# First attention layer: the sums over the keys as two rounded passes, both halves in the second step of the next batch

## The chip, the cores and the metric

The kernel runs on one core of one Trainium2 chip. TensorE (PE in the profile) multiplies matrices, VectorE (DVE), ScalarE (ACT) and GpSimd (POOL) do the elementwise work, and SyncE (SP) starts the transfers. Each engine takes its instructions in the order in which they are written, and engines wait for each other through semaphores. The metric is the device time of one execution in microseconds. Time before: 2079.07 us, the median of 3 runs (2076.28 to 2079.29).

## What is computed

The reference is a block of two layers on x of shape (16, 56, 256) with a context of shape (16, 1500, 128). Only the first cross attention matters here. For each of 16 batches, with 16 heads of 56 queries and 1500 keys:

```python
q = (layernorm(x) @ Wq).reshape(B, T_text, 16, 128)
k, v = context @ Wk, context @ Wv
attn = softmax(where(mask, q @ k.T / sqrt(128), -inf))   # over the 1500 keys
x = x + (attn @ v) @ Wo
```

The softmax divides by the sum of the exponentials over the keys. That sum is what the change is about. After this attention come a small mixing layer, a second cross attention and a mixture of experts.

## The kernel before

The loop over the batches `b` (16) has 12 steps `t` each. A step handles a tile of 125 keys against 896 query columns (16 heads of 56), in two halves of 448 columns. PSUM has three score banks in rotation (`slots`), three banks for side work (`side`) and two for the values (`psO`).

In step `t` of batch `b`:

- TensorE makes the scores of the next tile, `t + 1` (`scores_half`, L792 to L795): per half four matmuls of rounded operands (type F32R). Score operands are split in a high part (rounded, `chi`, `qhi`) and a low part (`clo`, `qlo`), and a fourth matmul adds the shift (`ones_r` by `shift`), which takes the largest score off. Then it multiplies the exponentials `P` of tile `t` by the context (`values_half`, L804, plain F32).
- Between these stand side jobs, in a fixed order: M (L826, scores of the batch after, for its maximum), T (transposes of it), N and A (L842 and L843, products from which the norms of the keys for the second layer are made). A side job may start only when the job three before it has been taken out of its bank by VectorE.
- ScalarE turns each half of the scores into exponentials (`exp`, L570), squares up the A jobs (`add_up`, L552, four pairs of instructions a job), rounds the operands of the batch after (`query_high`, `context_high`), and copies out the values of a batch at its end (`values_out`, L577).
- GpSimd adds the exponentials of the tiles up in `acc` (`add`, L641 for the first pair and L644), makes low parts (`context_low`, `query_low`), halves the N jobs (`halve`, L650), makes the shift of the batch after in step 10 (`make_shift`), and normalises (`normalise`, L657).
- VectorE takes M, T, N and A out of their banks (L711, L714, L738), adds up N (L747) and inverts the sums in steps 3 to 10 (`invert`, L753).

`acc` holds 125 partial sums for each query column. Over the 125 partitions TensorE adds them with a matmul by ones (`sums`, L812), plain F32, one for each half, and ScalarE copies the result to `den` (`sums_out`, L583). For batch `b - 1` this is done in batch `b`: the first half in step 0 behind the scores, the second at the head of step 1. On ScalarE the first copy stands in step 0 behind the exponentials, and the second behind the first A job of step 0. GpSimd's first `add` of batch `b` waits until both have been made, since it writes `acc` anew.

`ORDER` is the rotation of the three score banks, written out by hand: "S" stands for the scores of a step and half, "D" for the sums of the batch before, and "-" for a place left free. A bank is taken again three places later, and `wait_bank` makes TensorE wait for the reader of the place before: an exponential or a copy of a sum. The dispatch of ScalarE in a batch begins:

```python
for tile in tile_ahead(1, b, t):
    exp(*tile)
if t == 0 and b > 0:
    sums_out(b - 1, 0)
    norms_out(b - 1)
```

and goes on, through the conversions of the batch after where a step has them, to that step's A jobs.

Of the kernel before, what the change touches and what calls it, by code (L numbers as in the profile page):

```python
# [88 lines left out]
ORDER = [("S", 0, 0), ("S", 0, 1), ("S", 1, 0), ("S", 1, 1), ("D", 0, 0), ("D", 0, 1), ("-", 0, 0)]  # L89
ORDER += [("S", t, half) for t in range(2, NT) for half in range(2)]  # L90
# [66 lines left out]
def before_attention(nc, m, a, tag, sem):  # L157

    s = semaphores(sem, tag, LN_SEMAPHORES + ["ld_x", "ld_mask", "ld_const", "ld_ident", "ld_w0", "ld_w0_rest", "ld_wq0", "ld_wq1", "ld_wq2", "ld_wq3", "ld_w1", "ld_land", "ld_nat", "const", "ready",
                 "on_act", "on_dve", "f_hi", "g_hi", "x_hi", "mcount", "ctx_hi", "q_hi", "ctx_lo", "kept",  # L160
                 "side_pe", "side_dve"])
    with ExitStack() as ctx:
# [88 lines left out]
        def _(pool):  # L251
# [5 lines left out]
            pool.tensor_tensor(m.qlo0[:, :], q_first, m.qhi0[:, :].bitcast(F32), ALU.subtract).then_inc(s.kept, 1)  # L257
# [9 lines left out]
        def _(dve):  # L267
# [40 lines left out]
            def make_shift():  # L308

                dve.wait_ge(s.side_dve, len(PRE_SIDE))  # L310
                dve.wait_ge(s.ld_ident, 16)
                dve.tensor_tensor(m.shift0[:, :].rearrange("p (j c) -> p j c", c=TT),
                                  m.negmax[:, :].unsqueeze(2).to_broadcast([TT, QBLK, TT]),
                                  m.ident[0:TT, 0:TT].unsqueeze(1).to_broadcast([TT, QBLK, TT]),
                                  ALU.mult).then_inc(s.kept, 1)
# [125 lines left out]
def first_attention(nc, m, a, tag, sem):  # L441
# [3 lines left out]
        "scores", "probs", "pv", "acc", "den", "den_out", "inv", "o_raw", "o_done",  # L445
        "ld_wv", "ld_wo", "side_pe", "side_dve", "side_act", "half_sum", "sum_dve", "sum_act", "rk_pre"])
    NP = 3
    with ExitStack() as ctx:
# [12 lines left out]
        shift = [m.shift0, sb("shift1", [TT, QW], F32R)]  # L461
# [60 lines left out]
        def _(act):  # L522
# [55 lines left out]

            def sums_out(b, half):

                act.wait_ge(s.den, 2 * b + half + 1)
                need(act, s.o_done, 2 * b - 1 + half)
                act.activation(den[:, half, :], bank_of("D", 0, half)[:, 0:HALF], ACT.Copy).then_inc(s.den_out, 1)  # L583
# [5 lines left out]
            for b in range(B):  # L589
                for t in range(NT):  # L590
                    for tile in tile_ahead(1, b, t):
                        exp(*tile)
                    if t == 0 and b > 0:
                        sums_out(b - 1, 0)
                        norms_out(b - 1)
# [6 lines left out]
                    for n in STEP_JOBS[b, t]:  # L602
                        if JOBS[n].kind == "A":
                            add_up(n)
                        if n == first_of(b, "A") and b > 0:
                            sums_out(b - 1, 1)
# [14 lines left out]
        def _(pool):  # L621
# [7 lines left out]
            def query_low(b):  # L629
                pool.wait_ge(s.q_hi, b)  # L630
                if b >= 2:
                    pool.wait_ge(s.scores, 2 * NT * (b - 1))
                pool.tensor_tensor(qlo[b % 2][:, :], m.qs[:, b, :, :].rearrange("p h q -> p (h q)"),
                                   qhi[b % 2][:, :].bitcast(F32), ALU.subtract).then_inc(s.q_lo, 1)

            def add(b, t):
                pool.wait_ge(s.probs, 2 * (NT * b + t + 1))
                if t == 1:

                    need(pool, s.den, 2 * b)  # L640
                    pool.tensor_tensor(acc[:, :], P[0][:, :], P[1][:, :], ALU.add).then_inc(s.acc, 1)  # L641
                else:
                    pool.wait_ge(s.acc, (NT - 1) * b + t - 1)
                    pool.tensor_tensor(acc[:, :], acc[:, :], P[t % NP][:, :], ALU.add).then_inc(s.acc, 1)  # L644

# [22 lines left out]
            def make_shift(b):  # L668
# [3 lines left out]
                pool.tensor_tensor(shift[b % 2][:, :].rearrange("p (j c) -> p j c", c=TT),  # L672
# [4 lines left out]
            for b in range(B):  # L677
                for t in range(NT):
# [15 lines left out]
                    for n in STEP_JOBS[b, t]:  # L694
                        if JOBS[n].kind == "N":
                            halve(n)
            normalise(B - 2, 1)
# [4 lines left out]
        def _(dve):  # L702
# [13 lines left out]
            def turn_max(n):  # L716
# [3 lines left out]
                need(dve, s.shift, b - 1)  # L720
# [61 lines left out]
        def _(pe):  # L782
            def scores_half(b, t, half):
                if half == 0 and t == 0:
                    need(pe, s.ctx_lo, NLOW * b)
                    need(pe, s.q_lo, b)
                    need(pe, s.shift, b)
# [7 lines left out]
                pe.matmul(out, m.ones_r[:, :], shift[b % 2][:, cols], start=False, stop=True).then_inc(s.scores, 1)  # L795
# [12 lines left out]
            def sums(b, half):  # L808

                pe.wait_ge(s.acc, (NT - 1) * (b + 1))  # L810
                wait_bank(pe, b + 1, "D", 0, half)
                pe.matmul(bank_of("D", 0, half)[:, 0:HALF], m.ones[0:KT, :], acc[:, HALF * half:HALF * half + HALF],  # L812
                          start=True, stop=True).then_inc(s.den, 1)
# [34 lines left out]
            for b in range(B):  # L848
                for t in range(NT):
# [1120 lines left out]
def build(nc, a, out):  # L1970
    with ExitStack() as ctx:
# [26 lines left out]
        with ExitStack() as only:  # L1998
            for_first = lambda n, sh, dt: only.enter_context(nc.sbuf_tensor(n, sh, dt))
            m.ones_r = for_first("ones_r", [TT, KT], F32R)  # L2000
# [7 lines left out]
            m.shift0 = for_first("shift0", [TT, QW], F32R)  # L2008
# [54 lines left out]
```

## Time and profile before

| what | value |
|---|---|
| median of 3 runs | 2079.07 us |
| profiled execution, its own time | 2075.8 us |
| its span, first to last instruction | 2074.0 us |
| TensorE busy | 2044.6 us (99%) |
| VectorE, ScalarE, GpSimd busy | 1567.0, 1209.1, 1452.1 us |
| granted TensorE clock, mean | 0.999 |
| batches of the first attention | from 73 to about 1159 us |

In rows with times, the first number is the start from the beginning of the span and the second the duration, both in us; a bracket at the end gives the idle time of the engine before the row and what ended it. Matmuls overlap, so what one costs the stream is the time from its start to the start of the next, not its duration. A plain F32 matmul is recorded as two; the first of its records starts when it starts, and the instruction behind it appears early, so its cost is read over the following two starts.

### The profile page before, as it was taken

The page shows a single profiled execution, that of the slowest core. Times are in us where ns is not written, and L with a number is a line of the kernel's source. Part 1 is how long each engine was busy: PE and PEld are TensorE (multiplying, and loading weights), DVE is VectorE, ACT ScalarE, POOL GpSimd, SP SyncE. Part 2 cuts the span into 40 slices and gives each one's busy share as a digit, 9 for nine tenths or more (in the row PEclk, how much of TensorE's full clock was granted, in tenths as well). Part 3 has the DMA queues.
Part 4 walks back from the last instruction along what each step waited for, and adds up shares of the span by engine and source line. Part 5 has one row for each costly group of instructions (what it writes and reads, how often), then busy time and mean ns, then how long its engine had stood idle before and what let it go on. Part 6 is the DMA issues. An engine that isn't in the chain of part 4 may idle for free. (4 is left out here: it accounts for less than half of the span.)

```text
span 2074.0 us, 28056 instructions
## 1 busy us (share of the span) xinstructions
PE 2044.6 (99%) x8414; PEld 1511.9 (73%) x8414; DVE 1567.0 (76%) x2466; ACT 1209.1 (58%) x4202; POOL 1452.1 (70%) x1092
## 2 busy tenths in 40 slices
PE   8999999999999999999999999999999999999999
PEld 7777777777777777777777577666666666665898
DVE  4788988998889888988886677576766676752576
ACT  3676777777776777677767347544444444432443
POOL 1588888888888888888896255578787878761221
PEclk9999999999999999999999999999999999999999
DMA  4000000000000000000000320221212121101110
GB/s 138 31 16 16 31 30 16 26 21 31 29 18 16 31 30 16 16 31 30 16 16 36 121 74 1 63 60 31 60 30 60 30 60 30 45 1 54 39 54 26
DMA packets 16472, 76.59 MB, mean 37 GB/s; under 512 B 1986, under 2 KB 3506, under 8 KB 15314
## 3 DMA queue, kind: packets, MB, share of 16 engines
q1 hardware_dynamic: 16322, 74.81, 11.1%
q8 instruction: 67, 1.10, 0.2%
q14 instruction: 83, 0.68, 0.1%
HBM read 72.97 MB, written 0.92 MB: 36 GB/s over the span
## 5 line engine op out<-in xcount | busy, mean ns | idle before, releaser
L552 ACT ACTIVATE l_prod_act<-l_prod_act 125x128 f32<-125x128 f32 x1536 | 456.3, 299 | 298.3 <-DVE l_prod_act L738 293.3
L650 POOL TENSOR_TENSOR l_prod<-l_prod 125x256 f32<-125x256 f32 x384 | 280.8, 740 | 162.9 <-DVE l_prod L738 161.7
L1014 POOL TENSOR_TENSOR l_acc<-l_acc,l_probs 125x896 f32<-125x896 f32 x160 | 346.7, 2167 | 67.8 <-ACT l_probs L951 49.4
L951 ACT ACTIVATE l_probs<-l_scaled 125x896 f32<-125x896 f32 x192 | 182.8, 952 | 302.6 <-DVE l_scaled L1036 160.5
L1036 DVE TENSOR_TENSOR l_scaled<-l_slots,rk 125x896 f32<-125x896 f32 x192 | 206.9, 1084 | 180.8 <-PE l_slots L1112 180.7
L644 POOL TENSOR_TENSOR l_acc<-l_acc,l_probs 125x896 f32<-125x896 f32 x160 | 340.1, 2126 | 0.0
L552 ACT ACTIVATION_READ_ACCUMULATOR l_prod_act<-l_prod_act 125x1 f32 x1536 | 288.0, 187 | 0.0
L714 DVE SCALAR_TENSOR_TENSOR top<-l_side,mask_bias,top 125x448 f32<-125x448 f32 x330 | 217.6, 659 | 25.7 <-PE l_side L826 17.3
L570 ACT ACTIVATE l_probs<-l_slots,mask_bias 125x448 f32<-125x448 f32 x384 | 219.8, 618 | 1.2
L1110 PE MATMUL l_slots<-l_qhi,l_clo 128*125 128x448 f32 x384 | 203.0, 529 | 0.5
L842 PE MATMUL l_side<-norm_lo,l_chi 128*125 128x512 f32 x384 | 185.1, 482 | 0.1
L842 PE MATMUL l_side<-norm_lo,chi 128*125 128x512 f32 x384 | 180.9, 471 | 0.0
L804 PE MATMUL l_psO<-l_probs,spare 125*128 125x448 f32 x384 | 176.0, 539 | 0.0
L804 PE MATMUL l_psO<-l_probs,l_nat 125*128 125x448 f32 x384 | 175.9, 539 | 0.0
L738 DVE TENSOR_TENSOR l_prod<-l_side,xq 125x512 f32<-125x512 f32 x192 | 132.0, 687 | 50.6 <-PE l_side L843 48.9
L738 DVE TENSOR_TENSOR l_prod<-l_side,spare 125x512 f32<-125x512 f32 x192 | 132.0, 687 | 39.7 <-PE l_side L843 37.1
L1128 PE MATMUL l_psO<-l_probs,nat 125*128 125x448 f32 x384 | 160.5, 539 | 0.6 <-ACT qs L963 0.3
L1128 PE MATMUL l_psO<-l_probs,l_nat 125*128 125x448 f32 x384 | 160.3, 540 | 0.4
L747 DVE TENSOR_REDUCE l_msq<-l_prod 125x4 f32<-125x256 f32 x384 | 154.5, 409 | 0.0
L843 PE MATMUL l_side<-norm_hi,chi 128*125 128x512 f32 x384 | 151.4, 394 | 0.0
L843 PE MATMUL l_side<-norm_hi,l_chi 128*125 128x512 f32 x384 | 151.3, 394 | 0.0
L1111 PE MATMUL l_slots<-l_qlo,l_chi 128*125 128x448 f32 x384 | 140.5, 366 | 0.0
(278 smaller groups left out, 4926.0 us busy)
## 6 DMA issues: line engine op xcount, KB each, us to landing
land<-in_ctxT SPq DMA_DIRECT2D x32, 750.0 KB, 4.2
l_nat<-in_ctxN SPq DMA_DIRECT2D x16, 750.0 KB
post_we<-in_experts SPq DMA_DIRECT2D x20, 384.0 KB, 3.0
spare<-in_ctxN SPq DMA_DIRECT2D x8, 750.0 KB
nat<-in_ctxN SPq DMA_DIRECT2D x8, 750.0 KB
spare<-in_wo SPq DMA_DIRECT2D x2, 2048.0 KB, 7.3
spare<-in_wqT SPq DMA_DIRECT2D x4, 512.0 KB, 8.4
mid_fac<-in_factors SPq DMA_DIRECT2D x1, 2048.0 KB, 7.5
```

The costliest lines, as they stand in the source:

```text
L552: last = act.activation(whole, whole, ACT.Copy, accum_out=msq[:, t, 4 * g + c:4 * g + c + 1])
L570: act.activation(P[t % NP][:, HALF * i:HALF * i + HALF], bank_of("S", t, i)[0:KT, 0:HALF], ACT.Exp, bias=m.mask_bias[:, b, t:t + 1]).then_ ...
L644: pool.tensor_tensor(acc[:, :], acc[:, :], P[t % NP][:, :], ALU.add).then_inc(s.acc, 1)
L650: pool.tensor_tensor(buf[:, :, 0:C // 2], buf[:, :, 0:C // 2], buf[:, :, C // 2:C], ALU.add).then_inc(s.half_sum, 1)
L714: dve.scalar_tensor_tensor(top[:, cols], bank, bias, top[:, cols], ALU.add, ALU.max).then_inc(s.side_dve, 1)
L738: dve.tensor_tensor(to[:, :, :], bank, xt.unsqueeze(1).to_broadcast([KT, 4, C]), ALU.mult).then_inc(s.side_dve, 1)
L804: last = pe.matmul(psO[:, half, 0:HALF], nat[b % 2][:, t, :], P[t % NP][:, cols], start=t == 0, stop=t == NT - 1)
L842: pe.matmul(bank[0:KT, :], chi[b % 2][:, keys], m.norm_lo[:, cols], start=True, stop=False)
L843: last = pe.matmul(bank[0:KT, :], chi[b % 2][:, keys], m.norm_hi[:, cols], start=False, stop=True)
L1014: pool.tensor_tensor(acc[:, :], acc[:, :], P[t % NP][:, :], ALU.add).then_inc(s.acc, 1)
L1036: dve.tensor_tensor(scaled[t % 2][:, :].rearrange("p (a h q) -> p a h q", a=2, q=QS), src, rk.to_broadcast([KT, 2, H // 2, QS]), ALU.mult) ...
L1128: last = pe.matmul(psO[:, half, 0:HALF], nat[par][:, t, :], P[t % NP][:, cols], start=t == 0, stop=t == NT - 1)
```

## The change

The sums are made from rounded operands in two passes. ScalarE rounds `acc` to a high part (`sum_high`) into the buffer `qlo` of the batch just done; GpSimd takes the difference (`sum_low`) into that batch's `shift` buffer, which grows from 112 to 125 rows. TensorE adds ones by low and ones by high, in type F32R. Both halves are made one behind the other in step 1 behind the scores of tile 2, and ScalarE copies both out behind the exponentials of tile 2. `ORDER` has the two sums behind the scores of step 2. The last batch's sums stay as they were.

```diff
-ORDER = [("S", 0, 0), ("S", 0, 1), ("S", 1, 0), ("S", 1, 1), ("D", 0, 0), ("D", 0, 1), ("-", 0, 0)]
-ORDER += [("S", t, half) for t in range(2, NT) for half in range(2)]
+ORDER = [("S", t, half) for t in range(3) for half in range(2)] + [("D", 0, 0), ("D", 0, 1), ("-", 0, 0)]
+ORDER += [("S", t, half) for t in range(3, NT) for half in range(2)]
...
-        shift = [m.shift0, sb("shift1", [TT, QW], F32R)]
+        shift = [m.shift0, sb("shift1", [KT, QW], F32R)]
...
+            def sum_high(b):
+
+                act.wait_ge(s.acc, (NT - 1) * (b + 1))
+                act.wait_ge(s.scores, 2 * NT * (b + 1))
+                act.activation(qlo[b % 2][0:KT, :], acc[:, :], ACT.Copy).then_inc(s.sum_hi, 1)
...
                     for tile in tile_ahead(1, b, t):
                         exp(*tile)
+                    if t == 1 and b > 0:
+                        for half in range(2):
+                            sums_out(b - 1, half)
                     if t == 0 and b > 0:
-                        sums_out(b - 1, 0)
+                        sum_high(b - 1)
                         norms_out(b - 1)
...
                         if JOBS[n].kind == "A":
                             add_up(n)
-                        if n == first_of(b, "A") and b > 0:
-                            sums_out(b - 1, 1)
...
                 if b >= 2:
                     pool.wait_ge(s.scores, 2 * NT * (b - 1))
+                    pool.wait_ge(s.den, 2 * (b - 1))
...
                 if t == 1:
-
-                    need(pool, s.den, 2 * b)
+                    need(pool, s.shift, 2 * b)
                     pool.tensor_tensor(acc[:, :], P[0][:, :], P[1][:, :], ALU.add).then_inc(s.acc, 1)
...
+            def sum_low(b):
+
+                pool.wait_ge(s.sum_hi, b + 1)
+                pool.tensor_tensor(shift[b % 2][:, :], acc[:, :], qlo[b % 2][0:KT, :].bitcast(F32), ALU.subtract).then_inc(s.shift, 1)
...
                 need(pool, s.scores, 2 * NT * (b - 1))
-                pool.tensor_tensor(shift[b % 2][:, :].rearrange("p (j c) -> p j c", c=TT),
+                need(pool, s.den, 2 * (b - 1))
+                pool.tensor_tensor(shift[b % 2][0:TT, :].rearrange("p (j c) -> p j c", c=TT),
...
                     for n in STEP_JOBS[b, t]:
                         if JOBS[n].kind == "N":
                             halve(n)
+                    if t == 0 and b > 0:
+                        sum_low(b - 1)
...
-                need(dve, s.shift, b - 1)
+                need(dve, s.shift, 2 * b - 3)
...
-                    need(pe, s.shift, b)
+                    need(pe, s.shift, 2 * b - 1)
...
-                pe.matmul(out, m.ones_r[:, :], shift[b % 2][:, cols], start=False, stop=True).then_inc(s.scores, 1)
+                pe.matmul(out, m.ones_r[0:TT, 0:KT], shift[b % 2][0:TT, cols], start=False, stop=True).then_inc(s.scores, 1)
...
-                pe.wait_ge(s.acc, (NT - 1) * (b + 1))
+                cols, out = slice(HALF * half, HALF * half + HALF), bank_of("D", 0, half)[:, 0:HALF]
                 wait_bank(pe, b + 1, "D", 0, half)
-                pe.matmul(bank_of("D", 0, half)[:, 0:HALF], m.ones[0:KT, :], acc[:, HALF * half:HALF * half + HALF],
-                          start=True, stop=True).then_inc(s.den, 1)
+                if b == B - 1:
+                    pe.wait_ge(s.acc, (NT - 1) * B)
+                    pe.matmul(out, m.ones[0:KT, :], acc[:, cols], start=True, stop=True).then_inc(s.den, 1)
+                    return
+                pe.wait_ge(s.shift, 2 * b + 2)
+                pe.matmul(out, m.ones_r[0:KT, :], shift[b % 2][:, cols], start=True, stop=False)
+                pe.matmul(out, m.ones_r[0:KT, :], qlo[b % 2][0:KT, cols], start=False, stop=True).then_inc(s.den, 1)
...
-                    if t == 1 and b > 0:
-                        sums(b - 1, 1)
                     for half in range(2):
                         for tile in tile_ahead(1, b, t):
                             scores_half(*tile, half)
-                        if half == 1 and t == 0 and b > 0:
+                        if half == 1 and t == 1 and b > 0:
                             sums(b - 1, 0)
+                            sums(b - 1, 1)
                         side_jobs(len(jobs) // (4 - half))
```

`ones_r` grows to 128 by 128, and `shift0` to 125 rows (of which the maker of the first shift writes 112); a semaphore that nothing waited for (`kept`) goes.

## Rows read from the trace of the kernel before

**Rows 1.** Busy time by stretch, batches of the first attention; (x) counts instructions

```profile
73.00:1159.00 1086.00, 1085.84 (x4422) 814.03 (x4421) 942.51 (x1665) 781.19 (x3587) 904.52 (x800) 1.00 0.07 24
```

**Rows 2.** Timeline of TensorE, end of batch 1 and steps 0 and 1 of batch 2

```profile
208.31 0.37 PE L792 MATMUL l_slots<-qhi,clo 128*125 128x448 f32 x1
...
209.13 0.92 PE L812 MATMUL l_slots<-l_acc,ones 125*128 125x448 f32 x2
209.54 0.71 PE L826 MATMUL l_side<-l_qhi,l_chi 128*125 128x448 f32 x1
210.09 0.40 PE L842 MATMUL l_side<-norm_lo,chi 128*125 128x512 f32 x1
...
210.55 0.92 PE L804 MATMUL l_psO<-l_probs,spare 125*128 125x448 f32 x2
...
213.40 0.92 PE L812 MATMUL l_slots<-l_acc,ones 125*128 125x448 f32 x2
...
216.48 0.37 PE L826 MATMUL l_side<-l_qhi,l_chi 128*125 128x448 f32 x1
```

**Rows 3.** Timeline of ScalarE over the same stretch, from its last wait on

```profile
207.80 0.31 ACT L552 ACTIVATE l_prod_act<-l_prod_act 125x128 f32<-125x128 f32 x1 [0.25 <-DVE l_prod_act L738]
...
208.99 0.99 ACT L577 ACTIVATE qs<-l_psO,valid 128x896 f32<-128x896 f32 x1
...
211.95 0.53 ACT L583 ACTIVATE l_den<-l_slots 128x448 f32<-128x448 f32 x1
212.38 0.36 ACT L559 ACTIVATE rk<-l_msq 125x192 f32<-125x192 f32 x1
212.83 0.31 ACT L552 ACTIVATE l_prod_act<-l_prod_act 125x128 f32<-125x128 f32 x1
...
214.35 0.55 ACT L583 ACTIVATE l_den<-l_slots 128x448 f32<-128x448 f32 x1 [0.24 <-PE l_slots L812]
214.79 0.30 ACT L552 ACTIVATE l_prod_act<-l_prod_act 125x128 f32<-125x128 f32 x1
...
215.96 1.36 ACT L570 ACTIVATE l_probs<-l_slots,mask_bias 125x448 f32<-125x448 f32 x2
```

**Rows 4.** Timeline of ScalarE: a rounding copy of 896 columns and the next start

```profile
205.04 0.94 ACT L526 ACTIVATE l_qhi<-qs 128x896 fp32r<-128x896 f32 x1
205.88 0.51 ACT L535 ACTIVATE l_chi<-land 128x375 fp32r<-128x375 f32 x1
```

**Rows 5.** Groups by line and shape, ScalarE, batches of the first attention

```profile
L570 ACT ACTIVATE l_probs<-l_slots,mask_bias 125x448 f32<-125x448 f32 x384 | 219.8, 618 | 1.2
```

**Rows 6.** Timeline of all engines at the head of batch 0: a wait of TensorE

```profile
74.05 1.17 ACT L570 ACTIVATE l_probs<-l_slots,mask_bias 125x448 f32<-125x448 f32 x2
...
74.74 0.18 PEld L792 LDWEIGHTS l_slots<-qhi,clo 128*125 128x125 f32 x1 [0.41 <-ACT l_probs L570]
74.74 0.47 PE L792 MATMUL l_slots<-qhi,clo 128*125 128x448 f32 x1
...
75.04 0.36 PE L793 MATMUL l_slots<-qlo,chi 128*125 128x448 f32 x1
```

**Rows 7.** Timeline of VectorE and GpSimd over the same steps, in order of time

```profile
210.29 0.68 DVE L711 TENSOR_SCALAR top<-l_side,mask_bias 125x448 f32<-125x448 f32 x1 [0.35 <-PE l_side L826]
...
212.31 0.68 DVE L738 TENSOR_TENSOR l_prod<-l_side,spare 125x512 f32<-125x512 f32 x1
...
213.07 0.73 POOL L650 TENSOR_TENSOR l_prod<-l_prod 125x256 f32<-125x256 f32 x1 [2.31 <-DVE l_prod L738]
...
214.46 2.12 POOL L641 TENSOR_TENSOR l_acc<-l_probs 125x896 f32<-125x896 f32 x1 [0.66 <-PE l_slots L812]
...
219.69 0.73 POOL L650 TENSOR_TENSOR l_prod<-l_prod 125x256 f32<-125x256 f32 x1 [1.46 <-DVE l_prod L738]
```

**Rows 8.** Timeline of TensorE, ScalarE and GpSimd, steps 0 and 1 of batch 15

```profile
1089.22 0.99 PE L804 MATMUL l_psO<-l_probs,l_nat 125*128 125x448 f32 x2
...
1090.01 0.54 ACT L583 ACTIVATE l_den<-l_slots 128x448 f32<-128x448 f32 x1
...
1091.55 0.73 POOL L650 TENSOR_TENSOR l_prod<-l_prod 125x256 f32<-125x256 f32 x1 [2.29 <-DVE l_prod L738]
...
1094.58 0.40 PE L842 MATMUL l_side<-norm_lo,l_chi 128*125 128x512 f32 x1
```

More of the change, by code:

```diff
@@ L159, in before_attention @@
     s = semaphores(sem, tag, LN_SEMAPHORES + ["ld_x", "ld_mask", "ld_const", "ld_ident", "ld_w0", "ld_w0_rest", "ld_wq0", "ld_wq1", "ld_wq2", "ld_wq3", "ld_w1", "ld_land", "ld_nat", "const", "ready",
-                 "on_act", "on_dve", "f_hi", "g_hi", "x_hi", "mcount", "ctx_hi", "q_hi", "ctx_lo", "kept",
+                 "on_act", "on_dve", "f_hi", "g_hi", "x_hi", "mcount", "ctx_hi", "q_hi", "ctx_lo",
                  "side_pe", "side_dve"])
@@ L256, in _ @@
             pool.wait_ge(s.q_hi, 1)
-            pool.tensor_tensor(m.qlo0[:, :], q_first, m.qhi0[:, :].bitcast(F32), ALU.subtract).then_inc(s.kept, 1)
+            pool.tensor_tensor(m.qlo0[:, :], q_first, m.qhi0[:, :].bitcast(F32), ALU.subtract)
             pool.wait_ge(s.q_hi, 2)
@@ L311, in make_shift @@
                 dve.wait_ge(s.ld_ident, 16)
-                dve.tensor_tensor(m.shift0[:, :].rearrange("p (j c) -> p j c", c=TT),
+                dve.tensor_tensor(m.shift0[0:TT, :].rearrange("p (j c) -> p j c", c=TT),
                                   m.negmax[:, :].unsqueeze(2).to_broadcast([TT, QBLK, TT]),
                                   m.ident[0:TT, 0:TT].unsqueeze(1).to_broadcast([TT, QBLK, TT]),
-                                  ALU.mult).then_inc(s.kept, 1)
+                                  ALU.mult)
             dve.memset(m.ones[:, :], 1.0).then_inc(s.const, 1)
@@ L444, in first_attention @@
         "ld_land", "ld_nat0", "ld_nat1", "ctx_hi", "ctx_lo", "q_hi", "q_lo", "nat_hi", "xq", "shift",
-        "scores", "probs", "pv", "acc", "den", "den_out", "inv", "o_raw", "o_done",
+        "scores", "probs", "pv", "acc", "sum_hi", "den", "den_out", "inv", "o_raw", "o_done",
         "ld_wv", "ld_wo", "side_pe", "side_dve", "side_act", "half_sum", "sum_dve", "sum_act", "rk_pre"])
@@ L1999, in build @@
             for_first = lambda n, sh, dt: only.enter_context(nc.sbuf_tensor(n, sh, dt))
-            m.ones_r = for_first("ones_r", [TT, KT], F32R)
+            m.ones_r = for_first("ones_r", [C, C], F32R)
             m.mask_bias = for_first("mask_bias", [KT, B, NT], F32)
@@ L2007, in build @@
             m.top, m.negmax = for_first("top", [KT, QW], F32), for_first("negmax", [TT, QBLK], F32)
-            m.shift0 = for_first("shift0", [TT, QW], F32R)
+            m.shift0 = for_first("shift0", [KT, QW], F32R)
             m.xq = for_first("xq", [KT, NT, C], F32)
```

## The prediction

> **What bounds the kernel now.** I read the busy times by stretch first. Over the first attention's batches TensorE is busy 1085.84 of 1086.00 us at full clock, the other engines far less [rows 1]. So what is taken off TensorE's stream is gained, and whatever makes it wait is lost, as long as it stays the bound. The stream's costs come from starts. Four F32R matmuls of 448 columns take from 208.31 to 209.13, 0.205 us each. The plain F32 sum with one such matmul behind it takes from 209.13 to 210.09, so a sum costs 0.96 - 0.205 = 0.755 us [rows 2]. It is made 32 times, and 30 of them change.
>
> Then I read ScalarE's timeline at a batch's head, since the new order hangs on it. ScalarE last waits, 0.25 us for an A job, before the `add_up` at 207.80. That job comes from TensorE, so ScalarE's place is tied to TensorE's there. From there to 214.11 ScalarE goes without a pause: `values_out` and the conversions of the batch after have put it behind [rows 3]. Slack that its share of busy time suggests is absent at this one place. The heads of batches 1 to 14 run to the same pattern; batch 15 is calmer, as nothing is converted ahead.
>
> **The change, part by part.** I follow batch 2's head on the clock of before; TensorE has finished step 1's second score half at 216.48, both old sums included [rows 2]. That is the point to compare.
>
> *TensorE's work.* Two F32 sums (1.51 us) go. Four F32R matmuls (0.82 us) come. The gain in work is 0.69 us a head, 10.4 us over 15 heads.
>
> *Order on TensorE.* Without the old sums it would be at that point at 216.48 - 1.51 = 214.97. It would reach the values of tile 0 at 210.55 - 0.755 = 209.80. They need `values_out`, which ends at 208.99 + 0.99 = 209.98 [rows 2, 3]. What a wait costs is shown once: ScalarE's first exponential ends at 74.05 + 0.62 = 74.67, TensorE's matmul behind it starts at 74.74, and the next not after 0.205 but after 0.30 us [rows 5, 6]. So 0.07 us from end to start and 0.10 us of weight load laid bare. The values start effectively at 209.98 + 0.17 = 210.15, 0.35 us late, and the sums' place is reached at 215.32. The Trainium skill, page "TensorE: Matmul & The Clock Gate", section on the array's architecture, says that TensorE's queue pulls weight loads ahead of matmuls in flight. If it did so past a wait, the 0.10 us would vanish; the row at 74.74 shows load and matmul starting together, so the sum keeps it. By that rule the sum would end some 1.5 us lower.
>
> *The first half's wait: the low part.* `sum_high` starts on ScalarE where the first copy stood, 211.95. Its like, `query_high`, takes 0.94 us and lets the next start after 0.84 [rows 4]. It ends at 212.89. GpSimd comes to `sum_low` behind the second `halve` of step 0, at 213.07 before, released by VectorE's product at 212.31 [rows 7]. TensorE is 0.40 us early there, but VectorE has only 0.35 us of waiting to give back in that step [rows 7], so the halving moves to about 212.7 and ends the engine's turn at 213.4. `sum_low` is a GpSimd operation on 125x896 like `add`, 2.12 us [rows 7]: done at 215.5. TensorE makes the first half from 215.6 to 216.1 (0.30 + 0.205).
>
> *The second half's wait: its bank.* By the new `ORDER` the second sum goes into the bank of the scores of tile 2, first half, and `wait_bank` holds it until that exponential is out. On ScalarE that exponential stands behind both A jobs of step 0. Before, it started at 215.96. In between go the first copy (212.38 - 211.95 = 0.43 us) and the second with its wait (214.79 - 214.00 = 0.79; at 212.83 + 1.17 = 214.00 the first `add_up` would let the next start), together 1.22 us; `sum_high` brings 0.84 [rows 3, 4]. The 1.17 us of one `add_up` is 215.96 - 214.79. So it starts at 215.96 - 0.38 = 215.58 and its first half ends at 215.58 + 0.62 = 216.20 [rows 3, 5]. TensorE resumes at 216.27, with 0.30 + 0.205 us for the pair: 216.78. Against 216.48 the head is 0.30 us longer than before. TensorE has lost 0.35 us, then about 0.3 for the low part and about 0.3 for the bank and bare loads, more than the 0.69 gained.
>
> Behind the waiting matmul stand all side jobs and the values of step 1, so VectorE and the A jobs of ScalarE wait too. It can't be made up, because TensorE never idles later.
>
> *What is free.* GpSimd gets 2.12 us a head and loses a wait of 0.66; its first `add` ends near 217.5 instead of 216.6, and the 1.46 us of waiting before 219.69 takes that up [rows 7]. The first exponential that needs this `add` is that of tile 3, a whole step on. Were the cover gone, step 2's halvings would slip by about 1 us, and VectorE uses them three N jobs later. The two copies on ScalarE end near 217.5 (216.20 + 0.52 for the second exponential, then twice 0.43), and step 1's first A job comes behind a pair of score matmuls, an M job and its own product only after that. The bank of the first sum is asked for again by the scores of tile 3, in the next step. The new waits on `den` and `shift` in `query_low`, `make_shift` and `turn_max` look back most of a batch. The larger buffers and memsets cost nothing inside the loop. No transfer is added, and no load waits on anything that moves here.
>
> *Batch 15.* Before, TensorE's values wait for `values_out` already (0.99 where 0.92 is usual), so taking the first sum away there gives nothing; the point to compare is 1094.58 [rows 8]. GpSimd's halving at 1091.55 stays, `sum_low` runs from 1092.28 to 1094.40, the first half to 1094.97. ScalarE: 1090.01 + 0.84 + 0.45 + 1.17 = 1092.47, the second `add_up` 1.17 more, with 0.24 us for a wait of the kind in [rows 3]: 1093.88, so the exponential ends at 1094.5, in time. The second half ends at 1094.97 + 0.41 = 1095.38. That is 0.8 us longer.
>
> *Sum.* 14 x 0.30 + 0.8 = 5.0 us. On the profiled execution: span 2074.0 to 2079.0, its own time 2075.8 to 2080.8, 1.8 us above the span as before. The median of before lies 3.3 us above that execution; I add the 5.0 to the median: 2084.1 us, up 0.24%.
>
> **Bounds.** ScalarE's wake-up of TensorE costs from nothing to 0.17 plus the longest exposure that rows allow, a whole weight load of 0.18 in place of 0.10 [rows 6]: -0.17 to +0.08 a head, which gives 14 x 0.13 + 0.6 = 2.4 at the low end and 14 x 0.38 + 0.9 = 6.2 at the high end. The mean is near the shown case, which I take. `sum_low` has no row of its own; the nearest are `add` at 2.12 and the halving at 0.73. With 0.3 us more it would put the first half's end at 216.4, and the pair would end at about 216.8 all the same. With 1 us more the head grows by 0.5, another 7 us over the heads.
>
> **The rivals.**
>
> *The bank is free in time* (0.10). If the exponential of tile 2 did not hold the second sum, only the low part would: the pair ends at 216.1 + 0.205 = 216.3, 0.18 us before 216.48. 14 x -0.18 + 0.8 = -1.7: 2077.4 us, not slower. It decides from an exponential that ends before about 215.9, 0.3 us earlier than I have it. For it speaks only that the two copies leave ScalarE's step 0. Against it: both `add_up` still stand ahead, and no wait but 0.24 us was left on ScalarE there [rows 3].
>
> *The work saved is the time saved* (0.08). TensorE waits for nothing: -10.4 us, 2068.7. It needs the low part 0.6 us and the exponential 1.2 us earlier. For it: 99% of TensorE busy. Against: every row of the sum above.
>
> *The low part comes late* (0.08). `sum_low` beside VectorE's reads takes longer, or ScalarE's `sum_high` does and pushes the exponential: each 0.2 us beyond the margin is 0.2 a head, 15 x 0.2 = 3.0 us, so 2084.1 + 3.0 = 2087.1 us. For it: both are new in a stretch where ScalarE has no slack. Against: the same forms keep their durations elsewhere, 0.94 and 2.12 us.
>
> *TensorE's weight loads run ahead past the wait* (0.12). The head is 0.20 us longer, batch 15 0.7: 3.5 us, 2082.6, under the bound below. [...]
>
> **How the numbers follow.** The forecast has 0.62. A measurement of this kernel tells apart about 0.2%, 4.2 us. The forecast's own range, 2.4 to 6.2 us with the scatter of the runs (3 us between them) on top, lies about two thirds above 4.2. Slower by more than 0.2%: 0.62 x 0.70 + 0.08 + 0.12 x 0.3 = 0.55. Faster by more than 0.2%: the second rival, and a fifth of the first, 0.10. The rest, 0.35, is within 0.2%. The range 2077 to 2088 reaches to the first rival and to the late low part, and leaves out the second.
>
> **What would show it.** In the changed profile: F32R matmuls of the sums in pairs of 0.205 us; a wait of TensorE before the values of tile 0 on ScalarE's `values_out`, one before the first sum on GpSimd's low part, and one before the second sum on the exponential of tile 2, all told about 1.0 us a head where there was none. From one batch's head to the next it takes 0.3 us longer. TensorE busy falls by about 10 us while the span grows. GpSimd's wait for the sums is gone. If there is no wait on the exponential, the first rival holds. It would be wrong at large if ScalarE's work at the head ran otherwise than in these rows, or if the later end of step 1 were made up by something that waited for VectorE until now.

## The result and the profile after

The changed kernel takes 2081.36 us (median of 20 runs, 2079.53 to 2086.95) where the kernel before takes 2078.99 (20 runs). The ratio of the two is 1.0022, with a 95% interval of 1.0016 to 1.0028: slower by 4.6 us of 2079, and forecast were 5.0. The two medians themselves lie only 2.4 us apart, and the forecast median was 2084.1. The times go with the mean granted clock of the execution: of the changed kernel's 20, the four at 1.000 take 2079.5 to 2080.4 us and the three at 0.996 take 2084.8 to 2087.0; the kernel before, timed again beside e1 below, has five at 1.000 from 2073.6 to 2074.9, so at equal clock about 5.6 us lie between. The profiled execution has a span of 2080.9 us against 2074.0, 6.9 us more; that difference holds 1.7 us that are not the change's, see below.

The timeline of the changed kernel at the head of batch 2, the place of [rows 2], [rows 3] and [rows 7] (sum lines: L583 is now the rounding copy, L656 the low part, L832 and L833 the two passes, L846 the M job, L862 the first product of an N or A job, L819 the values, L726 VectorE taking an M job out of its bank):

```profile
208.31 0.30 ACT L552 ACTIVATE l_prod_act<-l_prod_act 125x128 f32<-125x128 f32 x1
...
209.83 0.31 ACT L552 ACTIVATE l_prod_act<-l_prod_act 125x128 f32<-125x128 f32 x1 [0.25 <-DVE l_prod_act L753]
...
211.02 0.99 ACT L577 ACTIVATE qs<-l_psO,valid 128x896 f32<-128x896 f32 x1
...
211.42 0.18 PEld L862 LDWEIGHTS l_side<-norm_lo,chi 128*125 128x125 f32 x1 [0.28 <-DVE top L726]
...
212.15 0.99 PE L819 MATMUL l_psO<-l_probs,spare 125*128 125x448 f32 x2
...
213.97 0.95 ACT L583 ACTIVATE l_qlo<-l_acc 125x896 fp32r<-125x896 f32 x1
...
215.44 2.13 POOL L656 TENSOR_TENSOR l_shift<-l_acc,l_qlo 125x896 fp32r<-125x896 f32 x1
...
217.18 0.36 PE L810 MATMUL l_slots<-shift,ones_r 112*125 112x448 f32 x1
...
217.63 1.13 ACT L570 ACTIVATE l_probs<-l_slots,mask_bias 125x448 f32<-125x448 f32 x2
...
217.72 2.12 POOL L648 TENSOR_TENSOR l_acc<-l_probs 125x896 f32<-125x896 f32 x1
217.72 0.44 PE L832 MATMUL l_slots<-l_shift,ones_r 125*128 125x448 f32 x1 [0.18 <-POOL l_shift L656]
...
218.00 0.36 PE L833 MATMUL l_slots<-l_qlo,ones_r 125*128 125x448 f32 x1
218.29 0.19 PEld L832 LDWEIGHTS l_slots<-l_shift,ones_r 125*128 125x128 f32 x1 [0.30 <-ACT l_probs L570]
218.29 0.47 PE L832 MATMUL l_slots<-l_shift,ones_r 125*128 125x448 f32 x1
218.40 0.19 PEld L833 LDWEIGHTS l_slots<-l_qlo,ones_r 125*128 125x128 f32 x1
218.60 0.37 PE L833 MATMUL l_slots<-l_qlo,ones_r 125*128 125x448 f32 x1
...
218.80 0.37 PE L846 MATMUL l_side<-l_qhi,l_chi 128*125 128x448 f32 x1
```

To lay this beside the rows of before, take the point to which ScalarE is tied, its last wait for an A job: 209.83 here, 207.80 there [rows 3]. Everything here is 2.03 us later for reasons that lie before this head. Taken off:

| step of the prediction | forecast | measured less 2.03 |
|---|---|---|
| values of tile 0 start, behind `values_out` | 210.05, and 0.10 for the bare load | 210.12 in the record |
| rounding copy on ScalarE | 211.95 | 211.94 |
| low part on GpSimd, start and time | 213.4, 2.12 | 213.41, 2.13 |
| the sums' place reached on TensorE | 215.32 | 215.36 (217.18 + 0.205) |
| first sum on TensorE | 215.6 | 215.69 |
| exponential of tile 2 on ScalarE | 215.58 | 215.60 |
| second sum on TensorE | 216.27 | 216.26 |
| the stream goes on | 216.78 | 216.77 |

Before, it went on at 216.48 [rows 2]. A head is 0.29 us longer although TensorE has 0.69 us less to do.

The waits of the changed kernel, over the first attention's batches; columns are the total, the number of times and the longest. They hold all three waits of the prediction, 14 or 15 times each, and one more, for VectorE (L726):

```profile
PEld l_slots L832 <- issue: 8.3, 15, 0.9
PEld l_psO L819 <- issue: 6.7, 15, 1.0
...
PEld l_slots L832 <- ACT l_probs L570: 4.2, 14, 0.3
PEld l_side L862 <- DVE top L726: 4.0, 14, 0.3
...
PE l_slots L832 <- POOL shift L656: 1.3, 7, 0.2
PE l_slots L832 <- POOL l_shift L656: 1.2, 7, 0.2
```

A lesson in reading stands here. TensorE's wait before the first sum is put down mostly to "issue", and its matmul row to only 0.18 us, because the matmuls before it are recorded as overlapping. The honest measure is again from start to start: the last score matmul starts at 217.18 and would let the next start at 217.39; it starts at 217.72.

**Where the 6.9 us of the span lie.** GpSimd's `make_shift` runs once a batch, late in it. These are its first and last in one buffer, of the kernel before and of the changed one (first and last start at the end):

```profile
L672 POOL TENSOR_TENSOR l_shift<-negmax,ident x8: 1682/1685/1685, 130.5 to 1077.2; 112x896 fp32r<-112x896 f32 x8
```

```profile
L685 POOL TENSOR_TENSOR l_shift<-negmax,ident x8: 1679/1680/1686, 132.2 to 1083.2; 112x896 fp32r<-112x896 f32 x8
```

Between them lie the heads of batches 1 to 14: 951.0 us for 946.7, so 4.3 us or 0.31 a head. At 132.2 the changed kernel is already 1.7 us late, before it has made a single sum. That is TensorE's clock in the preparation, and it is a property of the execution. Of the 1.7 us, 1.6 lie in one run of 24 products, recorded as 2.94 us before and 4.57 after. Its rows, before and after:

```profile
21.38 2.94 PE L406 MATMUL pre_bk<-pre_wkT 128*128 128x128 f32 x24 [0.94 <-DVE pre_fold_lo L348]
```

```profile
21.49 4.57 PE L406 MATMUL pre_bk<-pre_wkT 128*128 128x128 f32 x24 [0.94 <-DVE pre_fold_lo L348]
```

Busy times of the same stretch, before and after (the number behind POOL's count is the granted clock):

```profile
18.00:24.30 6.30, 4.09 (x34) 3.89 (x34) 6.20 (x21) 3.73 (x8) 0.00 (x0) 1.00 0.55 198
```

```profile
18.00:24.30 6.30, 3.96 (x22) 3.77 (x23) 6.19 (x20) 3.13 (x7) 0.00 (x0) 0.79 0.53 202
```

A mean of 0.79 says that for part of the stretch the lower of the two clock levels, 1.2 GHz, was granted (from 22 to 24 us the mean is 0.50): 22 matmuls for 34. From 18 to 22 us TensorE had been busy 1.67 us in this execution and 1.79 us in that of before, whose clock stayed. Other executions below start the attention's first matmul at 71.2 to 72.9 us, whatever the kernel; e4's starts it at 72.59 with a clock of 1.00 in this stretch, so a late start is not the clock each time. So I compare profiles by the stretch of the attention alone, from its first score matmul to the first of its closing matmuls. Before and after:

```profile
71.41 0.44 PE L792 MATMUL l_slots<-qhi,clo 128*125 128x448 f32 x1 [1.10 <-PEq L162]
```

```profile
L875 PE MATMUL l_side<-qs,spare x32: 537/539/542, 1154.7 to 1166.3; 128*128 128x448 f32 x32
```

```profile
73.11 0.44 PE L807 MATMUL l_slots<-qhi,clo 128*125 128x448 f32 x1 [1.09 <-PEq L162]
```

```profile
L894 PE MATMUL l_side<-qs,spare x32: 538/539/542, 1161.6 to 1173.2; 128*128 128x448 f32 x32
```

1083.3 us before, 1088.5 after: 5.2 us longer, 5.0 were forecast. Of these 4.3 are the fourteen heads, and 0.9 is left for batch 15, where 0.8 was forecast. The rows there, changed kernel:

```profile
1095.26 0.99 PE L819 MATMUL l_psO<-l_probs,l_nat 125*128 125x448 f32 x2 [0.60 <-ACT qs L577]
...
1098.28 2.14 POOL L656 TENSOR_TENSOR shift<-l_acc,qlo 125x896 fp32r<-125x896 f32 x1
...
1101.46 0.40 PE L862 MATMUL l_side<-norm_lo,l_chi 128*125 128x512 f32 x1
```

The values start 6.04 us behind those of before (1089.22), and the job behind the sums 6.88 us (1094.58) [rows 8]: 0.84 us longer, nearly all of it the wait for the low part, which is done at 1098.28 + 2.14 = 1100.42.

### The profile page after: what moved, and what is told of

It is laid out like the page before. It is cut to its first block and busy times, and to the rows that moved or that the text cites. A ratio compares the mean times of both kernels' runs of the same rounds, so it can differ in the third digit from the quotient of the medians.

```text
span 2080.9 us, 28101 instructions
## 1 busy us (share of the span) xinstructions
PE 2048.9 (98%) x8414; PEld 1510.9 (73%) x8414; DVE 1565.1 (75%) x2466; ACT 1218.1 (59%) x4217; POOL 1482.5 (71%) x1107
## 5 line engine op out<-in xcount | busy, mean ns | idle before, releaser
L862 PE MATMUL l_side<-norm_lo,l_chi 128*125 128x512 f32 x384 | 185.7, 483 | 0.1
L862 PE MATMUL l_side<-norm_lo,chi 128*125 128x512 f32 x384 | 181.5, 473 | 0.0
L819 PE MATMUL l_psO<-l_probs,l_nat 125*128 125x448 f32 x384 | 176.5, 540 | 0.6 <-ACT qs L577 0.6
L819 PE MATMUL l_psO<-l_probs,spare 125*128 125x448 f32 x384 | 176.5, 541 | 0.0
L753 DVE TENSOR_TENSOR l_prod<-l_side,xq 125x512 f32<-125x512 f32 x192 | 131.8, 687 | 50.7 <-PE l_side L863 49.0
L753 DVE TENSOR_TENSOR l_prod<-l_side,spare 125x512 f32<-125x512 f32 x192 | 131.8, 686 | 39.8 <-PE l_side L863 37.2
```

The lines of the kernel that those rows point to most:

```text
L753: dve.tensor_tensor(to[:, :, :], bank, xt.unsqueeze(1).to_broadcast([KT, 4, C]), ALU.mult).then_inc(s.side_dve, 1)
L819: last = pe.matmul(psO[:, half, 0:HALF], nat[b % 2][:, t, :], P[t % NP][:, cols], start=t == 0, stop=t == NT - 1)
L862: pe.matmul(bank[0:KT, :], chi[b % 2][:, keys], m.norm_lo[:, cols], start=True, stop=False)
```

## The experiments

Nine more kernels ran, one of them twice (e10 is e3 again), each timed over five rounds. Ratios are to the kernel before; the stretch is taken from each kernel's profile in the way just shown. Where a mean change per head is given, it comes from the starts of `make_shift`, again as above, over the fourteen heads.

| kernel | ratio, 95% interval | stretch, us | against before |
|---|---|---|---|
| before | 1 | 1154.7 - 71.41 = 1083.3 | |
| changed | 1.0022, 1.0016 to 1.0028 | 1161.6 - 73.11 = 1088.5 | +5.2 |
| e1, both sums later | 0.9972, 0.9963 to 0.9981 | 1152.0 - 72.67 = 1079.3 | -4.0 |
| e2, second sum later | 1.0011, 1.0002 to 1.0019 | 1157.2 - 71.37 = 1085.8 | +2.5 |
| e4, the place alone | 1.0021, 1.0012 to 1.0029 | 1161.9 - 72.59 = 1089.3 | +6.0 |
| e5, `values_out` ahead | 0.9989, 0.9981 to 0.9998 | 1155.3 - 72.90 = 1082.4 | -0.9 |
| e3, both edits | 0.9951, 0.9938 to 0.9963 | 1146.4 - 71.18 = 1075.2 | -8.1 |
| e6, kernel before, `values_out` ahead | 0.9997, 0.9988 to 1.0006 | 1154.7 - 71.41 = 1083.3 | 0.0 |
| e7, more on ScalarE | 1.0087, 1.0074 to 1.0099 | 1172.4 - 71.57 = 1100.8 | +17.5 |
| e8, more on ScalarE with both edits | 0.9967, 0.9955 to 0.9979 | 1146.5 - 71.17 = 1075.3 | -8.0 |
| e9, maxima first | 0.9968, 0.9956 to 0.9980 | 1148.6 - 71.55 = 1077.1 | -6.2 |
| e10, both edits again | 0.9952, 0.9939 to 0.9965 | 1146.6 - 71.41 = 1075.2 | -8.1 |

### e1: both sums later

```diff
                         if half == 1 and t == 1 and b > 0:
-                            sums(b - 1, 0)
-                            sums(b - 1, 1)
                         side_jobs(len(jobs) // (4 - half))
                     values_half(b, t, 0)
+                    if t == 1 and b > 0:
+                        sums(b - 1, 0)
+                        sums(b - 1, 1)
```

(The emptied `if` goes too.)

> The changed kernel with both sums moved on TensorE behind the first half of the values of step 1, some 1.4 us later; ScalarE and GpSimd as in the change. Theory A (TensorE's waits at the head eat the gain: 0.35 us on values_out, about 0.3 on the low part, about 0.3 on the bank held by the exponential of tile 2): the last two waits are gone, the first stays. 0.69 gained less 0.35 lost is 0.34 us a head over 14 heads, batch 15 level: about -4.7 us against the kernel before, ratio 0.9977, and 9.6 us under the changed kernel. Rival B (the added work itself costs: the rounding copy on ScalarE and the difference on GpSimd hold up side jobs): the move changes nothing, ratio near 1.002. Rival C (copies of the sums on ScalarE come later and push its add_up): slower than the changed kernel.

0.9972 and 4.0 us less in the stretch. The waits for the low part and for the bank are what cost; the passes themselves, ScalarE's rounding copy and GpSimd's difference are all still there, and the kernel is faster than before. Rival B falls. Rival C too: ScalarE now waits 9.9 us in all for the sums before it copies them, and nothing comes of it. By the starts of `make_shift` (131.8 to 1074.4) a head is 0.29 us shorter than before, where 0.34 was expected: the wait for `values_out` costs about 0.40 us and not 0.35.

### e2: only the second sum later

```diff
                         if half == 1 and t == 1 and b > 0:
                             sums(b - 1, 0)
-                            sums(b - 1, 1)
                         side_jobs(len(jobs) // (4 - half))
                     values_half(b, t, 0)
+                    if t == 1 and b > 0:
+                        sums(b - 1, 1)
```

> The changed kernel with only the second sum moved behind the first half of the values of step 1; the first stays where it must wait for the low part. Theory A: the wait for the bank and its bare weight load go, the wait for the low part stays: about +0.04 us a head against before, some 0.8 less in batch 15 than the changed kernel: 0 to +1.5 us, ratio 1.0000 to 1.0007. If the low part alone held the sums, it would be as the changed kernel, 1.0022; if the bank alone did, as the kernel with both later, 0.9977.

1.0011, between the changed kernel and e1 in the stretch (+2.5, where +5.2 and -4.0 lie around it). Both waits are real, and each holds part. It came out 1 us or more above the expectation, for two reasons. By the starts of `make_shift` (130.5 to 1078.9) a head is 0.12 us longer than before, where I had 0.04: in the rows of the changed kernel above, from GpSimd's end (215.44 + 2.13 = 217.57) to TensorE's start at 217.72 pass 0.15 us, not the 0.07 that I had from ScalarE. And batch 15 stays 0.8 us longer. I had expected it to lose that, without a reason: only the low part is waited for there, and this edit leaves that wait.

### e4: the place alone

```diff
-                pe.wait_ge(s.shift, 2 * b + 2)
-                pe.matmul(out, m.ones_r[0:KT, :], shift[b % 2][:, cols], start=True, stop=False)
-                pe.matmul(out, m.ones_r[0:KT, :], qlo[b % 2][0:KT, cols], start=False, stop=True).then_inc(s.den, 1)
+                pe.wait_ge(s.acc, (NT - 1) * (b + 1))
+                pe.matmul(out, m.ones[0:KT, :], acc[:, cols], start=True, stop=True).then_inc(s.den, 1)
...
-                        sum_high(b - 1)
                         norms_out(b - 1)
...
-                    if t == 0 and b > 0:
-                        sum_low(b - 1)
```

The first hunk holds for every batch. GpSimd's first `add` waits for `den` again, and the counts of `shift` are those of before.

> The place alone: both sums in step 1 behind the scores of tile 2 as in the change, but plain F32 from acc as before, without rounding copy and difference. Theory A: no work is saved; TensorE reaches the values of tile 0 early and waits 0.35 us for values_out, then nothing waits, since ScalarE's exponential of tile 2 is out before the second sum: +0.35 us a head, +0.8 in batch 15, 5.7 us, ratio 1.0027. If the place costs nothing (the waits come from the low part and the copy alone), ratio 1.0000.

1.0021, and +6.0 us in the stretch for 5.7. No work is saved or added on TensorE here, and still the kernel is slower: taking the sum out of step 0 only brings TensorE sooner to values that wait for `values_out`. The timeline of e4 (L816 is the values of tile 0, L825 the two sums) shows it with the 0.99 of a wait in place of 0.92:

```profile
211.70 0.99 PE L816 MATMUL l_psO<-l_probs,spare 125*128 125x448 f32 x2
...
216.94 1.67 PE L825 MATMUL l_slots<-l_acc,ones 125*128 125x448 f32 x4
```

The two sums go through in one block of four records; nothing waits between them.

### e5: `values_out` ahead of the last A job

```diff
                     for n in STEP_JOBS[b, t]:
+                        if t == NT - 1 and n == STEP_JOBS[b, t][-1]:
+                            values_out(b)
                         if JOBS[n].kind == "A":
                             add_up(n)
...
-                values_out(b)
                 if b + 2 < B:
                     context_high(b + 2, 1)
```

> The changed kernel with ScalarE's values_out one job earlier, ahead of the last A job of step 11, which takes the 0.25 us wait of ScalarE there away and ends values_out some 1.2 us earlier. The sums stay behind the scores of tile 2. Theory A: the wait before the values goes, but the waits behind it grow by as much; only the 0.25 us that ScalarE is ahead come off the exponential of tile 2: +0.05 us a head instead of +0.30, about -3.5 us against the changed kernel, ratio to before 1.0003 to 1.0008. A theory in which the values' wait is what counts would have -0.35 us a head against the changed kernel, ratio near 0.9997; one in which only the low part counts, no change from 1.0022.

0.9989 and 0.9 us less in the stretch: better than theory A had it by some 2.5 us, and near what the second theory would give. The head tells why. e5, timeline of batch 2:

```profile
208.53 0.69 DVE L754 TENSOR_TENSOR l_prod_act<-l_side,xq 125x512 f32<-125x512 f32 x1 [0.20 <-PE l_side L864]
...
216.69 1.14 ACT L570 ACTIVATE l_probs<-l_slots,mask_bias 125x448 f32<-125x448 f32 x2
...
216.91 0.44 PE L833 MATMUL l_slots<-l_shift,ones_r 125*128 125x448 f32 x1 [0.18 <-POOL l_shift L657]
...
217.19 0.36 PE L834 MATMUL l_slots<-l_qlo,ones_r 125*128 125x448 f32 x1
...
217.38 0.45 PE L833 MATMUL l_slots<-l_shift,ones_r 125*128 125x448 f32 x1
...
217.88 0.37 PE L847 MATMUL l_side<-l_qhi,l_chi 128*125 128x448 f32 x1
```

From the last A product to the exponential of tile 2 pass 216.69 - 208.53 = 8.16 us; in the changed kernel the same rows lie at 209.11 and 217.63, 8.52 us. The edit brought ScalarE 0.36 us forward, not 0.25; that is one size I had wrong. The bracket of 0.25 counts from the end of the record before, and ScalarE's records overlap. From start to start, the `add_up` ahead of the wait takes 209.83 - 208.31 = 1.52 us in the changed kernel, where one lets the next start after 1.17: the wait costs 0.35. The other size is batch 15, which is level with before here (1082.4 - 1083.3 = -0.9, and the fourteen heads alone are 945.8 - 946.7 = -0.9), while the changed kernel loses 0.84 us there. With ScalarE 0.36 us forward the bank comes free as the first sum ends: the second starts 0.19 us behind the matmul before it. What is left is the wait for the low part, from 216.37 + 0.205 to 216.91. So in the changed kernel it is not the values' wait that counts at a head: it is gone and TensorE still waits later. But as a result e5 doesn't part the two theories, since 0.36 us and the second theory's 0.35 are one number; e7 does.

### e3 and e10: both edits together

The edits of e1 and e5 in one kernel.

> Both edits together: both sums behind the first half of the values of step 1 on TensorE, and values_out ahead of the last A job of step 11 on ScalarE. Theory A: no wait is left at a head, so the whole 0.69 us of saved work counts, 15 heads, and batch 15 loses the wait it had before: -10.4 to -11.5 us against the kernel before, ratio 0.9945 to 0.9950. A theory in which something behind TensorE (VectorE, GpSimd) takes over as the bound gives less: no better than the kernel with both later alone, 0.9972.

> The kernel with both edits once more, as the neighbour of the one above on the same chip: ratio to before 0.9951 again, within 0.001.

0.9951 and, on another occasion, 0.9952: 10 us faster than before and some 15 faster than the changed kernel. This version beats both. e3, timeline of batch 2; TensorE takes both sums without a stop, and it is ScalarE that waits for them:

```profile
207.57 0.37 PE L808 MATMUL l_slots<-qhi,clo 128*125 128x448 f32 x1
...
209.22 0.92 PE L820 MATMUL l_psO<-l_probs,spare 125*128 125x448 f32 x2
...
216.24 0.36 PE L833 MATMUL l_slots<-l_shift,ones_r 125*128 125x448 f32 x1
...
216.43 0.98 ACT L589 ACTIVATE l_den<-l_slots 128x448 f32<-128x448 f32 x2 [0.79 <-PE l_slots L834]
216.44 0.37 PE L834 MATMUL l_slots<-l_qlo,ones_r 125*128 125x448 f32 x1
...
218.75 0.36 PE L808 MATMUL l_slots<-qhi,clo 128*125 128x448 f32 x1
```

The kernel before, timeline of batch 2, where step 0 begins and where the scores of tile 3 begin:

```profile
206.81 0.36 PE L792 MATMUL l_slots<-qhi,clo 128*125 128x448 f32 x1
...
220.03 0.36 PE L792 MATMUL l_slots<-qhi,clo 128*125 128x448 f32 x1
```

In the stretch it gains 8.1 us, though, not 10.4. By head: from the scores of tile 1's second half to those of tile 3 pass 11.18 us (207.57 to 218.75), before 11.72 (208.31 to 220.03), so 0.54 of the 0.69.

### e6: the control

The edit of e5 in the kernel before.

> The kernel before with values_out ahead of the last A job of step 11, sums untouched. Theory A: TensorE waits nowhere at the heads of batches 1 to 14, so nothing is gained there; only the 0.1 us wait of batch 15 goes: ratio 0.9995 to 1.0000. If the edit were a gain of its own, its gain in the kernel with both edits would not belong to the change: ratio near 0.998.

0.9997, and the stretch is the same to 0.1 us. What e3 gains is the change's own saving, set free; the reordering by itself is worth nothing.

### e7 and e8: one more copy on ScalarE

```diff
                 act.activation(qlo[b % 2][0:KT, :], acc[:, :], ACT.Copy).then_inc(s.sum_hi, 1)
+                need(act, s.o_done, 2 * b)
+                act.activation(den[0:KT, :, :], acc[:, :].rearrange("p (a c) -> p a c", a=2), ACT.Copy).then_inc(s.sum_hi, 1)
```

`sum_low` counts `sum_hi` by two and does not wait for the second; the copies of the sums and the next `add` wait for it. e7 has this in the changed kernel, e8 in e3.

> The changed kernel with one more copy of 896 columns on ScalarE at each head, behind the rounding copy (acc to den, which is overwritten by the sums later), so that the low part is not delayed and the exponential of tile 2 is, by 0.84 us. Theory A (that exponential holds the second sum): all of it shows: 14 x 0.84 + 0.5 = 12 us above the changed kernel, ratio to before 1.0080. If the low part alone held the sums, up to its margin, or if ScalarE had slack, 1.0022 to 1.0030.

> The same added copy on ScalarE in the kernel with both edits. Theory A: the exponential of tile 2 then ends at about the time at which TensorE comes to the second sum, so the copy is hidden: 0 to 1.5 us above the kernel with both edits, ratio to before 0.9945 to 0.9957. If ScalarE's time counted by itself, 12 us more, ratio near 1.0005.

e7: 1.0087, 1100.8 - 1088.5 = 12.3 us more in the stretch, and 12 expected. Each 0.84 us of ScalarE ahead of the exponential of tile 2 is 0.84 us of the kernel, while the low part comes as early as before. The pair of sums in e7 is torn apart, the second waiting:

```profile
217.02 0.44 PE L837 MATMUL l_slots<-l_shift,ones_r 125*128 125x448 f32 x1 [0.17 <-POOL l_shift L661]
217.30 0.36 PE L838 MATMUL l_slots<-l_qlo,ones_r 125*128 125x448 f32 x1
218.43 0.47 PE L837 MATMUL l_slots<-l_shift,ones_r 125*128 125x448 f32 x1 [0.78 <-ACT l_probs L570]
```

e8: the same copy costs 0.1 us in the stretch (1075.3 for 1075.2), and its profiled span is e3's, 2064.1 us. The timed ratio, 0.9967, lies above e3's by more than I expected, though the intervals meet (0.9955 to 0.9979 and 0.9938 to 0.9963). 12 us more would be 1.0009 and is excluded. A difference of a few us between e8 and e3 is neither shown nor excluded by the timing, and the profiles show none.

### e9: VectorE's last reductions behind its first job

```diff
                         side_job(n)
+                        if t == 0 and at == 0 and b > 0:
+                            for i in range(NBLK - LAG_N, NBLK):
+                                add_up(b - 1, i)
...
-                    if t == NT - 1:
-                        for i in range(NBLK - LAG_N, NBLK):
-                            add_up(b, i)
+            for i in range(NBLK - LAG_N, NBLK):
+                add_up(B - 1, i)
```

> The kernel with both edits, and VectorE's last three reductions of a batch (L763 there) moved behind its first job of the next batch, so that the first M job leaves its bank about 1 us earlier. In the kernel with both edits TensorE waits 0.27 us at each head for that bank (0.16 us of it lost), and the stretch of the first attention is 8.1 us shorter than before, not 10.4. Theory A': that wait is the missing part: 14 x 0.16 = 2.2 us below the kernel with both edits, the stretch 10.3 us shorter than before, ratio to before 0.9945. If something else makes up the difference, no change against the kernel with both edits.

The expectation was wrong: 0.9968, slower than e10 beside it, and 1.9 us more in the stretch than e3. The wait for the first M job's bank went, and two others came. e9, timeline of batch 2:

```profile
208.41 1.06 DVE L763 TENSOR_REDUCE l_msq<-l_prod 125x4 f32<-125x256 f32 x3
...
209.39 0.68 DVE L754 TENSOR_TENSOR l_prod<-l_side,spare 125x512 f32<-125x512 f32 x1
...
210.12 0.18 PEld L849 LDWEIGHTS l_side<-l_qhi,l_chi 128*125 128x125 f32 x1 [0.35 <-DVE l_prod L754]
...
210.71 0.18 PEld L865 LDWEIGHTS l_side<-norm_lo,chi 128*125 128x125 f32 x1 [0.41 <-DVE top L727]
```

The three reductions (1.06 us) now stand ahead of the N job, and TensorE waits for that bank and the next. VectorE's work for step 0 is eight jobs of about 0.60 us from start to start and these reductions at 0.98 (208.41 to 209.39), 5.8 us in all. TensorE's step 0 without the old sum is 213.40 - 206.81 - 0.755 = 5.8 us [rows 2]. At the head VectorE has as much to do as TensorE, so it has no slack; that the order of its work only chooses the place of the wait is what one order moved suggests, and is not shown beyond it. What was tested is this one order. Spreading the reductions over steps 0 and 1, where VectorE has waits again, was not tried.

## Why the prediction was right

**What bounds the kernel.** Right. TensorE does the same work in e3 as in the changed kernel, and 13 us lie between them (1075.2 and 1088.5): they are waits at the heads.

**Saved work.** 0.69 us a head. Not measured free of all waits in any kernel: e3 shows 0.54 of it, and the wait for VectorE that is left there takes the other 0.15.

**The values' wait for `values_out`.** Right in place, and a little too small: TensorE reaches the place of the sums at 215.36, where it would be at 214.97 without the wait, so 0.39 us and not 0.35. From the end of `values_out` (211.02 + 0.99 = 212.01) to TensorE's start at 212.15 pass 0.14 us, and I had 0.07. e4 shows the wait without any saved work: 5.1 of its 6.0 us are the fourteen heads (131.7 to 1083.5), 0.36 each. In the changed kernel the 0.04 us too few did not show, because the sums' times hang on GpSimd and ScalarE. One term was missed and made no difference here: TensorE did not reach the values freely at 209.80, because the first A job of step 0 waited 0.28 us for VectorE's first maximum. That wait lies under the one for `values_out` in the changed kernel and comes to light in e3. There the job that waits starts at 208.66 instead of 208.60 and its second product 0.33 us behind it instead of 0.23: about 0.15 of the 0.69 us a head. e9 fits with VectorE's load as the cause, since a new order of its work only moved the wait.

**The low part's wait.** Right: 215.69 for 215.6. The missing 0.09 is GpSimd's longer way to TensorE, 0.15 us and not 0.07. It hid behind the second sum's wait and shows only in e2.

**The second sum's bank.** Right, to 0.01 us (216.26 for 216.27), and shown by e7, where the delay passes through one for one. The first rival, that the bank is free in time, falls. e5 is what it would have been like: 0.36 us earlier on ScalarE, and the pair of sums runs nearly together. That the agreement is to 0.01 us is luck: the exponential's end is known only from a mean of 0.62 us.

**The bare weight load.** The row behind a wait repeats [rows 6]: from 218.29 to 218.60 pass 0.31 us, not 0.205. The Trainium skill, page "TensorE: Matmul & The Clock Gate", section on the array's architecture, has TensorE's queue pull weight loads ahead of matmuls in flight. By this case's rows it doesn't do so past a semaphore: load and matmul both start at 218.29. The page itself speaks of matmuls in flight and not of a wait, and there the trace agrees: the load at 218.40 starts while the matmul of 218.29 runs. The rival, which carried the rule past a wait, falls.

**What was called free** was free: the copies of the sums, GpSimd's 2.13 us a head, the later `add`, the new waits. e1 and e3 have all of it and are faster than before.

**Batch 15.** 0.84 us for 0.8, with the first half held by the low part and the second by nothing.

**TensorE's busy time.** Wrong, as a sign. I wrote that it falls by about 10 us while the span grows. It rose, from 2044.6 to 2048.9 us over the span and from 1083.1 to 1084.7 us over the stretch. Only 3.8 us of the stretch are shown as idle, though each head loses about 1.0 us to waits (217.39 to 218.80 is 1.41 us for 0.82 us of work, and 0.39 before it). The records of matmuls overlap, so waits of 0.3 us are largely covered by them. In e3, where these waits are gone, it is 1075.1 us.

**The sum.** 5.2 us in the profile's stretch and 4.6 by the ratio, for 5.0; the medians, 2.4 us apart, say less, and the median of 2084.1 us that I named lies 2.7 us above the measured one. It lay close to the bound of 0.2% (4.2 us), and the measured interval does not quite exclude a change under it (1.0016).

## What to carry to other kernels

Work taken off the engine that is always busy is worth only what the next semaphore lets through. Before counting it, walk the engine forward from the place of the saving to its next waits, with each releaser's own chain from a point that is tied to the same engine. A buffer rotation written by hand is such a wait: an instruction moved later takes the bank of a more recent tile, whose reader may stand behind other work. Where two waits lie one under the other, removing one shows the next; here three edits in turn met `values_out`, the low part and VectorE.

## What the runs showed of the hardware

From the end of the operation that is waited for to TensorE's start pass 0.05 us behind VectorE (210.69 + 0.68 = 211.37 to 211.42), 0.04 to 0.07 behind an exponential of ScalarE (217.63 + 0.62 to 218.29, and [rows 5, 6]), 0.14 behind ScalarE's `values_out` (212.01 to 212.15) and 0.15 behind GpSimd (217.57 to 217.72). It is not one figure for each engine that wakes it, and what sets it is not shown. Behind it come 0.08 to 0.10 us for a weight load that is no longer hidden (217.72 to 218.00 and 218.29 to 218.60, for 0.205). And the lower TensorE clock in the preparation comes and goes between executions: a mean of 0.79 in the changed kernel's stretch from 18.0 to 24.3 us, 1.00 in the kernel before, some 1.7 us of span that a comparison of two single profiles would have given to the change.
